# Moving a remainder matmul and the last layer one quarter of a step later on two engines

## The reference

```
x = x + conv3x3_mean(layernorm_over_channels(x))      # depthwise, every weight 1/9
t = tokens(x)                                         # one token per pixel, 256 numbers
t = t + ffn(layernorm(t))                             # then back to images
```

## Time and profile before

| | |
|---|---|
| median of three runs | 709.11 us |
| the profiled execution | 705.29 us |
| its span, first to last instruction | 703.5 us |
| TensorE busy | 506.6 us |
| VectorE busy | 526.0 us |
| ScalarE busy | 467.1 us |
| POOL busy | 296.2 us |
| mean granted TensorE clock | 0.898 |
| DMA, share of 16 engines | 79.8% |

### The profile page before, as it was taken

How to read it: one execution, slowest core, us unless ns; L and a number is a source line. 1 busy time by engine, 2 the same in 40 slices (tenths; PEclk the granted TensorE clock), 3 DMA queues, 4 the chain that set the end, 5 groups by cost and what they waited for, 6 DMA issues and landing times. The chain is left out here.

```text
span 703.5 us, 10091 instructions
## 1 busy us (share of the span) xinstructions
PE 506.6 (72%) x2040; PEld 207.6 (30%) x2040; DVE 526.0 (75%) x1495; ACT 467.1 (66%) x707; POOL 296.2 (42%) x644
## 2 busy tenths in 40 slices
PE   0036688888888888848788888858788878888850
PEld 0022233333333333313333332313333333333210
DVE  1579988888887887858888878868888888786220
ACT  0012788876777886737778877747777787688820
POOL 0024655544444545524445445524445544554100
PEclk9996899989988998969999989979999999899995
DMA  9599990994579916993459908930429039197999
GB/s 174 81 166 192 196 164 0 115 180 66 70 104 159 147 28 94 147 163 51 60 87 170 161 4 116 145 36 1 60 39 141 0 47 95 8 89 53 89 86 75
DMA packets 592607, 67.91 MB, mean 97 GB/s; under 512 B 592425, under 2 KB 592553, under 8 KB 592553
## 3 DMA queue, kind: packets, MB, share of 16 engines
q1 hardware_dynamic: 592552, 67.39, 79.8%
HBM read 33.83 MB, written 33.55 MB: 96 GB/s over the span
## 5 line engine op out<-in xcount | busy, mean ns | idle before, releaser
L779 ACT ACTIVATE xbuf<-xbuf,shift,gain (+1 forms) x256 | 222.4, 935 | 0.0
L557 DVE BATCH_NORM_STATS2 stat<-xbuf 128x6 f32 (+1 forms) x256 | 174.4, 685 | 21.6 <-DMA xbuf<-x 21.6
L657 POOL TENSOR_TENSOR nlo<-n,nhi 128x1024 f16<-128x1024 f32 x64 | 137.4, 2147 | 102.9 <-ACT nhi L762 100.5
L547 DVE SCALAR_TENSOR_TENSOR n<-xbuf,stat,ps 128x256 f32<-128x256 f32 x256 | 157.1, 651 | 6.4 <-DVE shift L476 6.2
L851 PE MATMUL ps<-h,w 128*128 128x512 f32 x256 | 140.6, 632 | 20.5 <-ACT h L746 17.4
L762 ACT ACTIVATE nhi<-n 128x1024 f16<-128x1024 f32 x64 | 67.7, 1057 | 119.8 <-DVE n L547 119.2
L574 DVE TENSOR_TENSOR xbuf<-ps,xbuf 128x512 f32 (+1 forms) x128 | 91.4, 714 | 66.1 <-PE ps L819 64.3
L667 POOL TENSOR_TENSOR over_bar<-xbuf,bar 128x536 f32<-128x536 f32 x32 | 42.3, 1322 | 210.4 <-DVE shift L476 210.4
L819 PE MATMUL ps<-nhi,band 128*128 128x512 f16 (+1 forms) x408 | 118.9, 409 | 13.1 <-POOL nlo L657 12.9
L819 PE MATMUL ps<-nlo,band 128*128 128x512 f16 (+1 forms) x408 | 116.7, 403 | 0.0
L843 PE MATMUL ps<-featT,w 128*128 128x512 f32 x128 | 77.4, 605 | 27.6 <-ACT featT L756 27.6
(11 more groups left out here) (81 smaller groups left out, 459.7 us busy)
## 6 DMA issues: line engine op xcount, KB each, us to landing
xbuf<-x SPq DMA_DIRECT2D x32, 512.0 KB, 6.9
xbuf<-x SPq DMA_DIRECT2D x16, 1024.0 KB, 11.2
out<-xbuf SPq DMA_DIRECT2D x32, 512.0 KB, 7.2
out<-xbuf SPq DMA_DIRECT2D x12, 1024.0 KB, 12.5
out<-xbuf SPq DMA_DIRECT2D x16, 256.0 KB, 8.1
consts<-cst SPq DMA_DIRECT2D x1, 168.5 KB, 2.4
b<-ba SPq DMA_DIRECT2D x8, 0.0 KB
b<-bs SPq DMA_DIRECT2D x8, 0.0 KB
```

The lines of the kernel that those rows point to most:

```text
L547: ins = v.scalar_tensor_tensor(n32[:, w // HALF, w % HALF, :], xview(par)[:, jc * CW + w, :], mean(k, w, w + 1), over(rn[:, w:w + 1], [P, C]),
L557: return v.bn_stats(stat[:, j % 4, at + 2 * s:at + 2 * s + 2, :].rearrange("p w n -> p (w n)"), xview(par)[:, w:w + 2, :].rearrange("p w c ...
L657: pool.tensor_tensor(nlo[:, at:at + HALF, :], n32[:, h, :, :], nhi[:, at:at + HALF, :], ALU.subtract).then_inc(lo_ready, 1)
L779: ins = act.activation(col, col, ACT.Identity, bias=shift[:, k, w:w + 1], scale=gain[:, k, w:w + 1])
```

## The change

On TensorE the remainder of layer 2 is issued in quarter 2 instead of quarter 1, and layer 3 in quarter 3 instead of quarter 2, each behind that quarter's convolution and tiles. On ScalarE the Relu of the remainder is issued in quarter 2 instead of quarter 1, behind that quarter's two Relus and ahead of its outputs. Every wait and every instruction stays as it is; ysb's copy stays in quarter 3.

```diff
                         act.activation(h2[:, GROUPS * (jc % 2) + i, :], ps[:, B_L2, :],
                                        ACT.Relu).then_inc(h2_ready, 1)
-                        if i == GROUPS - 1:
-                            act.wait_ge(l2r_done, c + 1)
-                            wait(act, l3_done, c)
-                            act.activation(h2r[:, :], ps[:, B_L2R, :], ACT.Relu).then_inc(h2r_ready, 1)
+                    if s == 2 and back:
+                        c = back[0]
+                        act.wait_ge(l2r_done, c + 1)
+                        wait(act, l3_done, c)
+                        act.activation(h2r[:, :], ps[:, B_L2R, :], ACT.Relu).then_inc(h2r_ready, 1)
...
                         pe.matmul(ps[:, B_L2, :], w2[:, :], h1[:, GROUPS * (jc % 2) + i, :], start=True,
                                   stop=True).then_inc(l2_done, 1)
-                        if i == GROUPS - 1:
-                            wait(pe, h2r_ready, c)
-                            wait(pe, y_read, c)
-                            for k in range(GROUPS):
-                                ins = pe.matmul(ps[32 * k:32 * k + 32, B_L2R, :], w2r[:, :],
-                                                h1[:, GROUPS * (jc % 2) + k, :], start=True, stop=True)
-                            ins.then_inc(l2r_done, 1)
                     if s == 2 and back:
+
+                        c, jc, par = back
+                        wait(pe, h2r_ready, c)
+                        wait(pe, y_read, c)
+                        for k in range(GROUPS):
+                            ins = pe.matmul(ps[32 * k:32 * k + 32, B_L2R, :], w2r[:, :],
+                                            h1[:, GROUPS * (jc % 2) + k, :], start=True, stop=True)
+                        ins.then_inc(l2r_done, 1)
+                    if s == 3 and back:
 
                         c, jc, par = back
```

## The result

The changed kernel takes 728.65 us (median of 4 runs, 726.02 to 732.7) where the kernel before took 709.1 in the same session: ratio 1.0274, 95% interval 1.0219 to 1.0329, slower. Forecast were 735 us and "slower". The profiled execution is 729.77 us with a span of 727.9, so 24.4 us more span than before.

A forecast was written before the change was run, and what follows sets the result against it. Before, ScalarE's chain of waits bounds the step at full clock, TensorE at low clock. Ordinary steps +20.5, early steps +4 and end +1.5 gave +26 us on 709.1: 735 us, whole range 708 to 748.

The forecast's parts named there:

- Part (1): Remainder matmuls on TensorE: their wait for VectorE's bank read goes; fast steps win nothing, slow ones up to 2.1 us.
- Part (2): ScalarE, quarter 2: the remainder's Relu adds an unhidden 0.48 us, making ScalarE's loop of waits 18.58 us.
- TensorE's ring: Once-a-step chain of waits from addition through ScalarE's Relus, layer 2, layer 3, convolution 1 to addition: 18.87 us.
- Part (3): TensorE, quarter 3: layer 3 between layer-2 tile and convolution 1 decides; step 18.87 us, 0.77 above the fast step.
- gated tile: Quarter 3's layer-2 tile on TensorE, which waits for ScalarE's Relus; TensorE forecast to stand 2.9 us before it.
- Part (4): TensorE: after a 2.9 us wait the lower clock falls on layer 2, layer 3, convolution 1, costing 1.5 us.
- low stretch: Time with TensorE at the lower clock, 1.2 GHz, about 3.5 us; a step with one was forecast at 20.4 us.
- The sum: 22 ordinary steps, 18 at 20.4 and 4 at 18.87: 442.7 us against 422.2; with the other steps +26 us.
- A: Rival, chance 0.09: TensorE's clock does not fall in the new line despite the longer wait; -4, 705 us.
- B: Rival, chance 0.08: the removed wait was the bound, TensorE early everywhere, ScalarE's loop sets 18.58 us; 697 us.
- C: Rival, chance 0.10: two slow-clock stretches between layer 2 and convolution 1 in half of 18 steps; +13, 748 us.
- D: Rival, chance 0.04: what convolution 4 wins in slow steps is given back before convolution 1; 709 us.

The follow-up runs named there:

- e4: Kernel before with only the remainder moved, to quarter 2 ahead of the layer-2 tile; layer 3 and the remainder's Relu stay as before: 681.59 us.
- e6: Kernel before with quarter 1's layer-1 matmul issued four times instead of once: 686.72 us.
- e2: Changed kernel with layer 3's eight matmuls on h2 moved ahead of quarter 3's layer-2 tile, the two on h2r still behind it: 695.28 us.
- e3: Changed kernel with remainder and layer 3 each ahead of their quarter's layer-2 tile, and the remainder's Relu back in quarter 1: 677.87 us.
- e1: Changed kernel with ScalarE as before, the remainder's Relu staying in quarter 1: 793.84 us.
- e9: e4 with layer 3 also moved, from quarter 2 to quarter 3 behind the layer-2 tile: 739.61 us.
- e8: Changed kernel with quarter 3's layer-1 matmul issued ten times and quarter 2's five times: 703.23 us.
- e5: Changed kernel with quarter 3's layer-1 matmul issued five times instead of once: 712.66 us.

## Why the prediction was right, point by point

- **Part (1), the wait on L491.** Right: in the changed kernel it is gone, and so, in the 24 steps, is VectorE's wait at the fourth addition. e4, which shortens it from 2.2 to 0.7 us a step and adds nothing to a ring, shows what can be won there, 28 us. The split between "hidden at full clock" and "paid at the lower clock" is shown by e6, which keeps the wait and takes the clock's fall away: its steps are 18.1 to 18.3 us, as e4's, so away from the loop edges nothing is left to win from the wait but the clock.
- **Part (2), h2r's 0.48 us in ScalarE's ring.** Right in size where it can be seen: e2's steps are 18.6, e3's, with the Relu back in quarter 1, 18.1. In the changed kernel it does not show: TensorE's ring (18.87 in the sum) is the longer one, though part (2) says that nothing hides it. That leaving it in quarter 1 would cost 65 us more (e1) I had not seen; there the change on ScalarE is needed by the change on TensorE.
- **Part (3), layer 3 between the gated tile and convolution 1.** Right, and shown from both sides: e2 takes 33 us off, e9 puts 58 on. At a clock kept up the ring is 18.9 to 19.3 us (e8) against 18.87 forecast. The places named are there: tile gated by ScalarE, wait 2.81 us (2.9 forecast), addition 2.01 us late (0.3 to 2).
- **Part (4), the clock.** Right in mechanism: with the waits filled, 25 us of the changed kernel's 728.65 disappear (e8). But the kernel before loses nearly as much to it, 22 to 24 us (e6). So of the 19.5 us that the change costs, some 16.5 us are the longer ring (703.23 - 686.72, both filled, of two sessions) and about 3 us are clock; the recorded sum holds the same split, 22 x 0.77 = 17 and the rest of its 20.5. My reasoning that a low stretch is partly hidden before and bare after was true for a stretch that lies on the ring: 20.48 - 19.04 = 1.4 us in the changed kernel (19.04 is a step that came behind a stretch off the ring), against 1.07 before. Over the 24 steps it comes to little: filling the waits gives back 19.0 us before (470.93 to 451.94) and 21.4 after (489.58 to 468.20), and the time at the lower level, by the trace's granted clock, is about the same in both, 99 and 96 us. The length of that one wait does not settle whether the clock falls: before, TensorE stands 2.2 us at L857 in every ordinary step, in those with a low stretch and in those without (the mean of 2.36 us had two waits of 5 us at the loop edges in it). The Trainium skill (TensorE: Matmul & The Clock Gate, section HAM oscillation) counts half of the throttled duration as lost, by which 3.4 us would cost 1.7, an estimate; the steps here pay 1.07 before and 1.4 after, less than that half. That the rest lies beside other engines' work I have not shown. The loop that section describes waits 3 to 5 us for DMA in each round, which the prediction left out; the waits in the changed kernel's steps are 2.1 and 2.8 us, for ScalarE. The mean clock did not fall below 0.88 as I had named for a sign; it is 0.90 in the 24 steps.
- **The sum.** The 22 ordinary steps take 489.58 - 22.16 - 24.72 = 442.7 us, which is the figure forecast, but not by its composition: 7 steps are at 18.7 to 19.1 us, one at 19.35, 11 at 20.0 to 20.6 and 3 at 21.6 to 22.0. I had 4 that keep the full clock and 18 that do not; in fact there is a low stretch in each of the 24 steps. What counts is where it lies: when it misses the line from the gated tile to convolution 1, the next addition waits 0.5 us or less and that step is short (but for one of 20.04 us behind a loop edge); when it lies on the line, the addition waits 2.0 us; and behind three stretches of double length on the line it waits 3.1 to 3.5. That the steps add up to the forecast 442.7 us is luck. Two neighbouring steps, the double stretch that begins in the first, and the addition behind it:

```profile
168.87:187.88 19.01, 14.06 (x58) 5.28 (x56) 15.89 (x45) 14.19 (x22) 9.28 (x20) 0.87 0.06 11
187.88:209.53 21.65, 18.28 (x73) 7.25 (x70) 15.91 (x46) 14.42 (x23) 9.27 (x20) 0.88 0.64 90
183.00:189.80 6.80, 5.80 (x13) 1.45 (x14) 2.86 (x8) 4.85 (x9) 1.63 (x6) 0.50 0.56 79
...
191.23 0.72 DVE L574 TENSOR_TENSOR xbuf<-ps,xbuf 128x512 f32 x1 [3.09 <-PE ps L820]
```

- **The steps around them.** The loop edges gave 1.9 us back (0 forecast, -1 each as bound), the three early steps cost 4.9 (4), the two late ones 2.7 (1.5). In the profiled runs the loss is 24.4 us against 26.
- **The level.** 735 against 728.65: 1.6 us are this sum (26 against 24.4), 3.8 the distance of the profiled run before from its median, which I carried over and which did not recur: the profiled run after lies 1.1 us above its median. A chance offset of one execution should have been shrunk.
- **The rivals.** A falls with the low stretches (the row at 0.51, and the steps above 20 us), B with the first addition's wait, which comes in nearly every step, D with the interval. C's double stretch is there, on the line in three steps where C had half of 18.

## What to carry to other kernels

When work moves on an in-order engine, look at what it lands between: layer 3 went from a place where the engine was merely late to the one between a wait for another engine and the result that closes the loop, and there each of its microseconds counts. The same matmuls one tile earlier, in the wait itself, cost nothing (e3 against e4), and the clock stays higher besides (0.957 of the span against 0.895 in the changed kernel). An edit can be right in one part (here the remainder, worth 28 us once it also goes ahead of its tile) and wrong in another that hides it; try the parts alone.

## What the runs showed of the hardware

- Adding up to thirteen useless matmuls a step made the kernel faster, on both sides (709.1 to 686.72 us, 728.65 to 703.23 us). What they buy is the granted clock: 0.89 to 0.98 and 0.90 to 0.99 over the 24 steps.
- The repeated float32r matmuls of layer 1 follow one another at 0.24 us (nine from 410.21, the tenth at 412.39 in e8), where the profile page of the kernel before has a mean of 0.605 us for one of them: a group's mean duration was no price for one more of them, which is why e5 filled less than counted.
- In the changed kernel nine of the steps from 371 us on are 20.4 to 20.6 us, and low stretches in them come every 20.5 us (408.25, 428.75, 449.25). The step length and the fall of the clock seem to hold each other there; I did not test it.
